# Attention scores from fp32 operands in four groups of 32 partitions, and a new order of TensorE's work within a step

## The reference

```
# x, ctx: (8, 256, 512); 16 heads of 16 rows; layernorm over the last axis
q = Wq @ layernorm(x) + bq;  k = Wk @ ctx + bk;  v = Wv @ ctx + bv
dot  = einsum('bhdt,bhds->bhts', q, k) / 4            # 512 x 512 a head
dot  = mask * dot - (1 - mask) * 1e6
x    = x + einsum('bhts,bhds->bhdt', softmax(dot) * mask, v)
h    = layernorm(x)                                   # 2048 tokens of 512
logits = h @ gate_w.T; the two best of 8 experts, weights w
x    = x + sum over the two of  w * (silu(h @ g) * (h @ u)) @ w2
```

## Time and profile before

| | us |
|---|---|
| median of three runs | 974.7 |
| lowest, highest | 970.87, 975.07 |
| the profiled execution's own time | 971.9 |
| its span, first to last instruction | 970.1 |

### The profile page before, as it was taken

The page is one execution under the profiler, slowest core; times in us unless marked ns, Lnnn a source line. Parts: engine busy times, 40 slices in busy tenths (PEclk is TensorE's granted clock), DMA queues, the critical chain, the costliest instruction groups (busy, mean ns, idle before and its releaser), DMA issues. The chain is left out here.

```text
span 970.1 us, 12844 instructions
## 1 busy us (share of the span) xinstructions
PE 820.0 (85%) x3737; PEld 366.6 (38%) x3738; DVE 547.9 (56%) x1055; ACT 316.5 (33%) x615; POOL 377.2 (39%) x396
## 2 busy tenths in 40 slices
PE   2078999999988998999899986159999999999994
PEld 1022323333333332333333322135555555555552
DVE  3186878788878877878788852403223232323322
ACT  0003556455545655555566675000000000000000
POOL 5643445457545754755474232401111111111111
PEclk9577999899999999999999998569999999999998
DMA  4553656566756856646664423322535365352332
GB/s 118 173 166 110 190 171 193 182 201 195 224 164 185 254 168 189 219 146 184 185 185 139 134 81 120 130 66 55 150 58 146 64 152 141 68 150 59 65 57 40
DMA packets 83567, 137.69 MB, mean 142 GB/s; under 512 B 13880, under 2 KB 39800, under 8 KB 83520
## 3 DMA queue, kind: packets, MB, share of 16 engines
q1 hardware_dynamic: 67792, 107.97, 36.7%
q0 software_dynamic: 7744, 17.86, 9.4%
q10 hardware_dynamic: 7984, 11.28, 4.0%
HBM read 77.34 MB, written 59.36 MB: 141 GB/s over the span
## 5 line engine op out<-in xcount | busy, mean ns | idle before, releaser
L731 DVE TENSOR_REDUCE mx<-tile 128x2 f32<-128x1024 f32 x256 | 309.0, 1217 | 67.8 <-PE tile L1005 64.8
L629 ACT ACTIVATE pr<-sc 128x512 f32<-128x512 f32 x512 | 268.8, 602 | 212.4 <-PE sc L992 209.5
L1005 PE MATMUL tile<-qk 97*128 97x512 bf16 x512 | 160.6, 397 | 43.8 <-DMA qk<-mrow_d 22.3
L1305 POOL DMA_INDIRECT out_dram<-y,ids x36 | 56.1, 1558 | 282.5 <-DVE ids L1230 278.4
L992 PE MATMUL sc<-qk 100*128 100x512 bf16 x512 | 156.2, 386 | 5.0 <-ACT pr L629 3.4
L1021 PE MATMUL pvb<-pr,vp 128*32 128x512 f32 x1024 | 141.3, 625 | 0.0
L1355 PE MATMUL dp<-wring,at 128*128 (+1 forms) x216 | 102.2, 609 | 13.4 <-DVE at L1240 13.4
L1285 ACT ACTIVATE sg<-gp 128x352 f32<-128x352 f32 x36 | 16.7, 463 | 291.7 <-PE up L1334 291.7
L1005 PEld LDWEIGHTS tile<-qk 97*128 97x128 bf16 x512 | 36.6, 98 | 182.5 <-DVE mx L731 75.9
L554 POOL TENSOR_SCALAR parts<-qkf 128x512 bf16<-128x512 f32 x32 | 48.3, 1511 | 140.5 <-DVE qkf L827 139.4
L1334 PE MATMUL gp<-wring,xtile 128*128 x288 | 94.0, 470 | 2.1 <-DVE meta L1221 2.1
(11 more groups left out here) (120 smaller groups left out, 742.2 us busy)
## 6 DMA issues: line engine op xcount, KB each, us to landing
qk<-stack_d SPq DMA_DIRECT2D x32, 768.0 KB
stack_d<-parts SPq DMA_DIRECT2D x32, 384.0 KB, 2.6
wring<-w_dram SPq DMA_DIRECT2D x32, 352.0 KB, 7.0
xl<-routed_d ACTq DMA_DIRECT2D x38, 257.0 KB, 2.7
stack_d<-parts SPq DMA_DIRECT2D x32, 256.0 KB, 2.9
pv_d<-ov SPq DMA_DIRECT2D x32, 256.0 KB, 3.5
xin<-x_dram SPq DMA_DIRECT2D x16, 256.0 KB, 5.8
cin<-ctxt_dram SPq DMA_DIRECT2D x8, 512.0 KB, 6.2
```

Source lines behind the costliest of these rows:

```text
L629: nc.scalar.activation(pr[s % 2][:, j, :], sc[(32 * u + 4 * s + j) % NSC][:, :], ACT.Exp, scale=SCALE).then_inc(exped.sem, 1)
L731: dve.tensor_reduce(mx[:, half(w), 2 * j:2 * j + 2], t[:, :, :], X, ALU.max, negate=True).then_inc(drained.sem, 1)
L1005: last = nc.tensor.matmul(t[:, i, :], qs[half(w)][0:RAW_ROWS, h, c * P:c * P + P], ks[half(w)][0:RAW_ROWS, h, :], start=True, stop=True)
L1305: pool.indirect_dma_start(out, bass.IndirectOffsetOnAxis(ap=ids[:, k, :], axis=0), y[:, k, :], None, compute_op=ALU.add).then_inc(y_added, 16)
```

## The change

q and k stay fp32. Each projected q and k tile has four groups of 32 partitions, and one transfer per group copies it to the 16 first partitions of the same group of `qk`, two sets of four heads beside each other; the mask bias is partition 16 of a group, the maximum partition 17. A score matmul so contracts 18 fp32 rows of one group of 32, a raw one 17, and the four heads of a set lie in four different groups. `part`, `keep_split`, `stack` and `split_maxima` go; `move` (five transfers a unit) comes; `qk` has three buffers instead of two; the maxima are transposed in fp32 and placed by two transfers.

TensorE's order in a step becomes: scores of heads 0 and 1 (groups 0 and 1) with the first raw pair (groups 2 and 3); filler; second raw pair (groups 0 and 1) with scores of heads 2 and 3 (groups 2 and 3); product of the step before. The list of tile jobs and VectorE's order follow: the filler's tile now lies between the two raw pairs.

```diff
-PAIRS = [(0, 0), (0, 1), (0, 2), (1, 0), (1, 1), (2, 0)]
-
-RUNS = [(0, 3, 0), (3, 2, 1), (5, 1, 2)]
-BIAS_ROW = D * len(PAIRS)
-MAX_ROW = BIAS_ROW + 1
-RAW_ROWS = BIAS_ROW + 1
-ALL_ROWS = MAX_ROW + 3
+GROUP = 32
+BIAS_ROW, MAX_ROW = D, D + 1
+RAW_ROWS, ALL_ROWS = D + 1, D + 2
...
+NQK = 3
...
+def raw_of(m):
+
+    return m // 8, m % 8 // 2, 2 - 2 * (m % 2)
+
+
 def tile_events(n):
     ev = []
     for s in range(8):
         max_ = [("max", m) for m in pairs_of(n, s)]
-        if s == 7:
-            ev += max_[:1] + ["ranks"] * has(n - 2) + max_[1:] + ["k"] * has(n + 3)
-            continue
-        ev += max_
+        ev += max_[:1]
...
+        if s == 7:
+            ev += ["ranks"] * has(n - 2) + ["k"] * has(n + 3)
+        ev += max_[1:]
     return ev
...
+        mrow_d = dram("mrow_d", [B, 2, 2, T], F32)
...
-        rest = sb("rest", [P, 2, T])
-        parts = sb("parts", [P, 2, 3, T], BF16)
-        qk = [sb(f"qk{i}", [P, 2, UH, T], BF16) for i in range(2)]
-        qs, ks = ([t[:, side] for t in qk] for side in range(2))
+        qk = [sb(f"qk{i}", [P, 2, 2, T]) for i in range(NQK)]
...
-        mxr = sb("mxr", [P, 32])
-        mxp = sb("mxp", [P, 3, 32], BF16)
-        mxt = sb("mxt", [96, P], BF16)
+        mx = sb("mx", [P, 2, 2, 4, 4])
+        mxt = sb("mxt", [32, P])
         den = sb("den", [P, 32])
...
-
-                if (due := scored.at(w - 2, (4 * g + 3, 3))) is not None:
+            def move(u):
+
+                w = u + 2
+                sp.wait_ge(drained.sem, drained.at(u - 1, "k"))
+
+                if (due := scored.at(w - NQK, (7, 3))) is not None:
                     sp.wait_ge(scored.sem, due)
-                heads = slice(4 * g, 4 * g + 4)
-                sp.dma_start(qk[half(w)][0:BIAS_ROW, :, heads, :],
-                             stack_d[half(w), :, :, :, heads, :].rearrange("s i d h t -> (i d) s h t")
-                             ).then_inc(stacked[g].sem, 16)
-                sp.dma_start(qk[half(w)][BIAS_ROW:BIAS_ROW + 1, :, heads, :],
-                             mrow_d[batch(w):batch(w) + 1]).then_inc(stacked[g].sem, 16)
-
-            def keep_split(u, side):
-
-                w = u + 3 - side
-
-                if (due := stacked[1].at(w - 3, "g")) is not None:
-                    sp.wait_ge(stacked[1].sem, due)
-                sp.wait_ge(split[side].sem, split[side].at(u, 3))
-                for first, n, part in RUNS:
-                    if side == 0:
-                        src = parts[:, 0, part:part + 1, :].broadcast_to([P, n, T])
-                    else:
-                        src = parts[:, 1, 0:n, :]
-                    sp.dma_start(stack_d[half(w), side, first:first + n].rearrange("i d h t -> (d h) i t"), src
-                                 ).then_inc(split_kept[side].sem, 16)
+                dst = qk[w % NQK]
+                for j in range(4):
+                    at = GROUP * j
+                    sp.dma_start(dst[at:at + D, :, :, :], qkf[at:at + GROUP, half(w), :, :]).then_inc(moved.sem, 16)
+                sp.dma_start(dst[BIAS_ROW::GROUP, :, :, :],
+                             mrow_d[batch(w):batch(w) + 1].broadcast_to([4, 2, 2, T])).then_inc(moved.sem, 16)
 
             def store_product(u, g):
...
+                pool.wait_ge(ones_made, i + 1)
             for h in range(2):
-                pool.memset(ks[h][96:128, :, :], 1.0).then_inc(ones_made, 1)
-                pool.wait_ge(ones_made, 2 * h + 1)
                 pool.memset(vp[h][:, :, :, D:], 1.0).then_inc(ones_made, 1)
-                pool.wait_ge(ones_made, 2 * h + 2)
+                pool.wait_ge(ones_made, NQK + h + 1)
             pool.wait_ge(const_loaded, CONST)
 
...
 
-                if j == 0 and (due := maxsplit.at(u - 1, "r1")) is not None:
-                    dve.wait_ge(maxsplit.sem, due)
+                if j == 0 and (due := ready.at(u - 1, "maxT")) is not None:
+                    dve.wait_ge(ready.sem, due)
                 t = tile_of(u, ("max", j))
-                dve.tensor_reduce(mx[:, half(w), 2 * j:2 * j + 2], t[:, :, :], X, ALU.max, negate=True
+                g, c, first = raw_of(j)
+                dve.tensor_reduce(mx[:, half(w), g, first:first + 2, c], t[:, :, :], X, ALU.max, negate=True
                                   ).then_inc(drained.sem, 1)
...
-                dve.tensor_copy(mxt[:, :], t[:, 0, :].bitcast(BF16)[0:96, 0:P]).then_inc(drained.sem, 1)
+                dve.tensor_copy(mxt[:, :], t[0:32, 0, 0:P]).then_inc(drained.sem, 1)
...
-                if (due := split[side].at(u - 2 + side, 1)) is not None:
-                    dve.wait_ge(split[side].sem, due)
+                if (due := moved.at(w - 4, "m")) is not None:
+                    dve.wait_ge(moved.sem, due)
...
                 maximum(u, 6)
                 token_stats(u, 0)
+                values_out(u)
                 maximum(u, 7)
                 token_stats(u, 1)
-                values_out(u)
 
                 maximum(u, 8)
                 token_normalize(u, 0)
@@ -859,37 +784,33 @@
                 maximum(u, 10)
                 batch_stats(u, 0)
                 reciprocals(u, 0)
+                projection_out(u, 0)
                 maximum(u, 11)
                 batch_stats(u, 1)
                 reciprocals(u, 1)
-                projection_out(u, 0)
 
                 maximum(u, 12)
                 maximum(u, 13)
 
                 maximum(u, 14)
                 normalize(u)
+                choose(u, 0)
                 maximum(u, 15)
-                choose(u, 0)
-                split_maxima(u, 0)
                 choose(u, 1)
-                split_maxima(u, 1)
                 choose(u, 2)
-                split_maxima(u, 2)
                 choose(u, 3)
-                split_maxima(u, 3)
 
                 maximum(u, 0)
                 choose(u, 4)
+                maxima_out(u)
                 maximum(u, 1)
                 choose(u, 5)
-                maxima_out(u)
 
                 maximum(u, 2)
                 rows_of(u, 0)
+                projection_out(u, 1)
                 maximum(u, 3)
                 rows_of(u, 1)
-                projection_out(u, 1)
...
@@ -983,27 +903,27 @@
             def scores(u, s, j):
 
                 g, c = s // 4, s % 4
-                h = 4 * g + j
                 if s == 0 and j == 0:
                     pe.wait_ge(maxrows.sem, maxrows.at(u - 1, "m"))
 
                 if (due := exped.at(u, (s, j), back=NSC)) is not None:
                     pe.wait_ge(exped.sem, due)
-                nc.tensor.matmul(sc[(32 * u + 4 * s + j) % NSC][:, :],
-                                 ks[half(u)][0:ALL_ROWS, h, c * P:c * P + P],
-                                 qs[half(u)][0:ALL_ROWS, h, :], start=True, stop=True
-                                 ).then_inc(scored.sem, 1)
+                both = qk[u % NQK][GROUP * j:GROUP * j + ALL_ROWS, g, :, :]
+                nc.tensor.matmul(sc[(32 * u + 4 * s + j) % NSC][:, :], both[:, 1, c * P:c * P + P],
+                                 both[:, 0, :], start=True, stop=True).then_inc(scored.sem, 1)
 
             def raw_scores(u, m):
 
                 w = unit_of(u, m)
-                if m % 8 == 0:
-                    pe.wait_ge(stacked[m // 8].sem, stacked[m // 8].at(u, "g"))
+                if m == 0:
+                    pe.wait_ge(moved.sem, moved.at(u, "m"))
                 t = slot(u, ("max", m))
+                g, c, first = raw_of(m)
                 for i in range(2):
-                    h, c = (2 * m + i) // 4, (2 * m + i) % 4
-                    last = nc.tensor.matmul(t[:, i, :], qs[half(w)][0:RAW_ROWS, h, c * P:c * P + P],
-                                            ks[half(w)][0:RAW_ROWS, h, :], start=True, stop=True)
+                    at = GROUP * (first + i)
+                    both = qk[w % NQK][at:at + RAW_ROWS, g, :, :]
+                    last = nc.tensor.matmul(t[:, i, :], both[:, 0, c * P:c * P + P], both[:, 1, :],
+                                            start=True, stop=True)
                 last.then_inc(ready.sem, 1)
...
-                pe.wait_ge(maxsplit.sem, maxsplit.at(u, "p2"))
+                pe.wait_ge(drained.sem, drained.at(u, ("max", NPAIR - 1)))
                 t = slot(u, "maxT")
-                nc.tensor.transpose(t[:, 0, :].bitcast(BF16)[0:96, 0:P],
-                                    mxp[:, :, :].rearrange("p i m -> p (i m)"), idb[:, :]
-                                    ).then_inc(ready.sem, 1)
+                nc.tensor.transpose(t[0:32, 0, 0:P], mx[:, half(u + 1), :, :, :].rearrange("p g j c -> p (g j c)"),
+                                    idf[:, :]).then_inc(ready.sem, 1)
...
@@ -1100,17 +1019,6 @@
                         scores(u, s, 0)
                         scores(u, s, 1)
                     for m in todo[:1]:
-                        raw_scores(u, m)
-                    if has(u):
-                        scores(u, s, 2)
-                        scores(u, s, 3)
```

(47 more changed lines are left out.)

71 lines of the change are left out of this document (11 added, 60 removed).

## The result

The changed kernel takes 1297.76 us (median of four runs, 1297.54 to 1300.05) against 972.79 (969.32 to 975.07) for the kernel before: ratio 1.335, 95% interval 1.33 to 1.34. The forecast was 1046 in a range of 1010 to 1112. Slower was right. The size was not: +325 us, where +71 was forecast (1046 against the 974.7 known then).

A forecast was written before the change was run, and what follows sets the result against it. TensorE was taken to set the pace, with VectorE near behind. Profiled 971.9 us plus 84 for longer units minus 13 in the lead-in gave 1043, or 1046 against the median; range 1020 to 1070, with queueing loads 1010 to 1112.

The forecast's parts named there:

- lead-in: Stretch before the first scores: raw pairs from about 29, 18 us earlier, serialized fillers add 5; net -13 us.
- The rate: Score matmuls on TensorE: four row groups run side by side, a set of four 0.96 us with one load exposed.
- plain step: Attention step without filler (0 and 2): second set ends at 2.78, array change 0.09, product 1.00; 3.87 us against 2.85.
- queueing loads: Rival: weight loads of a set's four heads come one after another, last head 0.32 us late; 1100 us; chance 0.20.
- two or one group at a time: Rival: row groups work two at a time (about 1230 us) or not at all (over 1500); chance 0.14 together.
- bank and slot waits: Within a step: head 3 waits for its score bank until 1.82 us, second raw pair for its tile slot until 2.40.
- signature: Signs in the trace: score matmuls with ScalarE as releaser, raw ones with VectorE, each about 1 us a step.
- Step 5: Attention step with the logits, which wait 2.38 us for ScalarE's copy; 5.43 us in all.
- Step 6: Attention step with the maxima transposes as filler, second raw pair waiting for its slot until 2.40; 4.45 us.
- VectorE fits in: VectorE in each unit: 16 reductions of 1.22 us are 19.5, and it loses the splits' two casts.
- Hidden waits: Rival: second set runs on at 0.96 us, lead-in gives its full 18; 970 to 980 us; chance 0.04.
- A faster stream: Rival: fp32 in a row group streams faster than on the whole array, set of 0.45 us; about 920; chance 0.04.

The follow-up runs named there:

- `blocks`: Changed kernel plus gapless matmul blocks behind attention, whole-array ones between: four groups of 18 or 32 rows, two groups, one group; sets of four 0.86 us each.
- `rise`: Changed kernel plus dense blocks behind attention, each set of four (18, then 32 rows) started after pairs at half clock; 18-row sets took 1.71 us each.
- `between`: Changed kernel, 18 rows, with the product moved between a step's two sets of scores and the filler to the end; 1137.22 us, ratio 1.164.
- `xt_early`: Changed kernel, 18 rows, with only ScalarE's copy of the token transpose moved behind the second exp of step 4; 1177.28 us, ratio 1.2139.
- `rows32_xt`: Changed kernel with all 32 rows of a group contracted and ScalarE's token copy moved behind the second exp of step 4; 1051.42 us, ratio 1.0815.
- `keeper`: Changed kernel, 18 rows, with one whole-array fp32 matmul, result overwritten, added in the waits of steps 4 to 7; 1248.70 us, ratio 1.2863.

## Why the prediction was wrong, point by point
- **The failed step** is one that never stood as a step: "at full clock in nearly every slice" was read as a property of the chip in mid-run and carried over to the kernel after. Each duration in the sum is one at full clock. What would hold or lose the clock with the new matmuls was not asked, though the lead-in's 0.68 in the earlier trace rows showed that it isn't given. In its place the runs show dense sets of 18 rows that hold a full clock but don't raise it from half (`blocks`, `rise`), and a clock that falls once a unit: in the changed kernel behind the waits of steps 4 and 5, in `between` without an idle gap before it. By ratios, of 326 us: 18 instead of 32 rows 194 (1.335 less 1.1356), the wait for ScalarE's copy with the fall behind it 53 (1.1356 less 1.0815), the rest 79 (1.0815), about what the forecast priced, at 71. The first two depend on each other: taken in the other order, by `xt_early`, the copy is worth 118 and the rows 129.
- **The rate** was right: four groups side by side, 0.86 a dense set, and 3.86 a plain step at full clock. The Trainium skill, "TensorE: Matmul & The Clock Gate", Part 3, gives 3.07 times for four row tiles; the dense block shows 4 x 0.86 / 0.86 = 4.0, and a set with one load exposed, at the 0.96 of the forecast, 3.6. The rivals with queueing loads and with two or one group at a time are refuted by the starts within 0.02. The price of two at a time was also mis-added: even 16 units of 46 come to about 1190 in all, not 1230.
- **The bank and slot waits** were right in place and size at full clock: in `rows32_xt` steps 0, 2, 3, 4, 7 are within 0.16 and step 1 within 0.12, and unit 1 of the changed kernel takes 35.31 for 34.9. Their signature was partly wrong. Score matmuls hardly show ScalarE as releaser, since raw passes of the same set keep the engine busy.
- **Step 5 was mis-sized.** I let only the logits wait for the copy. But the first raw pair of step 5 takes the slot of the token transpose, two jobs before it, so it waits too, 1.12 + 0.60 + 0.60 = 2.32 after the step's start (515.52 to 517.82: 2.30), and the second pair waits its 2.40 behind that: 2.32 + 2.40 + 2.05 = 6.8 at full clock where I had 5.43. I had the rule ("a job takes the slot of the job two places before it") and didn't apply it to this job.
- **Step 6 was mis-sized** by 0.67, for the cast ahead of the reduction. "VectorE fits in" counted its time, not the place of a single long instruction.
- **The lead-in** gave less: the first raw pair at 31.48 (29 forecast), since the five issues took 3.3 and not 2.3 and landed 3.9 later, and from there 49.07 to the first scores (42 forecast) with the clock at 0.58. First scores at 80.55, for 84.23 before: 4 us gained, not 13. Unit 0, which has no token work either, took 49.27 at a mean clock of 0.69, not 34.9.
- **The other two rivals.** Hidden waits: none were. A faster stream: a dense set of 0.86 excludes it.
- **What stays open:** why four groups of 18 rows hold but don't raise the clock, what number of rows between 18 and 32 would do, and how much waiting it takes to bring the clock down. No run here varied these. The k projection of 3.78 us, whole-array work too, doesn't raise the clock in the changed kernel, where a wait of 1.25 stands before it. In `between`, without that wait, most rises of mid-run come about 1 us behind it (in the unit shown it ends at 456.25, and the first passes of full-clock length start at 457.20), and in `keeper`, with an added matmul before it, at its end. What counts there was not tested.
## What to carry to other kernels
Ask of every change to a matmul's form whether TensorE still earns its full clock with it, and read the granted clock beside the busy share, which rose here while the engine ran most of the attention at half speed. If fewer rows than a group's 32 are used, zero rows up to 32 cost no time a matmul here and were worth 191 us. Where little behind it raises the clock again, a short wait costs many times its own length; but a list without idle gaps doesn't by itself keep the clock, as `between` shows. And the slot rule must be applied to every job around a moved one.
## What was not expected of the hardware
- Sets of four fp32 matmuls with 18 rows each: 0.86 us from a full clock, but 1.71 for 82 us on end from half, 100% busy; sets with 32 rows came from half to full in the same run.
- Two groups of 18 rows or one, 100% busy, run down to half clock (0.52 and 0.53 over 78 us).
- The 18-row kernel of `between` loses its full clock once a unit though TensorE is busy 459.91 of 460 us.
- Row groups overlap fully: 48 dense sets of four in 41.4 us, what 96 passes of 0.43 take one after the other.
